# Deformable 3x3 convolution: offsets in 27 products over four strips, four sampling banks, bias in constant rows

## What is computed

```python
x = x + _L0_conv_ref(_gn(x), Wa, ba, Wb, bb, Wg, bg, Wo, bo)
x = x + _L1_conv_ref(_gn(x), w_off, b_off, w_def)
# _L1_conv_ref(x, w_off, b_off, w_def), K = 3, so 9 taps and 18 offsets:
x = jax.nn.relu(x)
offset = conv3x3(x, w_off) + b_off[None, :, None, None]
py = base_y + off[:, :, 0]          # off = offset as (B, 9, 2, H, W)
px = base_x + off[:, :, 1]
samp = _bilinear_gather(x, py, px)  # every tap of every pixel at its own place
out = einsum('bckhw,ock->bohw', samp, w_def)
```

## Time and profile before

| | before |
|---|---|
| median of 3 runs | 1659.01 us (1657.56 to 1660.0) |
| profiled execution, its own time | 1660.34 us |
| its span | 1658.2 us |
| PE busy | 1566.1 us (94%) |
| DVE, ACT, POOL busy | 1183.6, 1033.9, 919.9 us |
| mean granted clock of PE, share of full | 0.982 |

### The profile page before, as it was taken

How to read it: one execution, slowest core, us unless ns; L and a number is a source line. 1 busy time by engine, 2 the same in 40 slices (tenths; PEclk the granted TensorE clock), 3 DMA queues, 4 the chain that set the end, 5 groups by cost and what they waited for, 6 DMA issues and landing times.

```text
span 1658.2 us, 27065 instructions
## 1 busy us (share of the span) xinstructions
PE 1566.1 (94%) x8915; PEld 987.9 (60%) x8916; DVE 1183.6 (71%) x2218; ACT 1033.9 (62%) x1820; POOL 919.9 (55%) x555
## 2 busy tenths in 40 slices
PE   5999999948999999999999999999999999999998
PEld 3778787714555555555555555555555555555554
DVE  5888888745667777776777767777766777767764
ACT  2555555535666666666666666666666666666663
POOL 3555555616555555555555555555555555555561
PEclk9999999958999999999999999999999999999999
DMA  5333333245766666666666666666666666665550
GB/s 145 99 117 117 117 114 114 76 149 167 213 186 180 177 177 177 176 180 179 180 180 183 184 177 176 193 177 184 183 186 180 178 184 182 181 181 171 166 153 26
DMA packets 190601, 268.03 MB, mean 162 GB/s; under 512 B 19710, under 2 KB 128279, under 8 KB 190487
## 3 DMA queue, kind: packets, MB, share of 16 engines
q1 hardware_dynamic: 190486, 266.60, 55.0%
HBM read 188.33 MB, written 78.18 MB: 161 GB/s over the span
## 4 chain that ended last, share of the span: by engine, by line
PE 72%; issue 11%; POOL 6%; DVE 4%; SPq 3%; ACT 3%; DMA 1%; POOLq 0%; DVEq 0%; ACTq 0%
PE bank L827 29%; PE pair L796 22%; PE pair L873 9%; POOL samples_hi L1567 4%; PE pair L845 4%; PE bank L845 3%; DVE samples_lo L1359 2%; ACT samples_hi L1048 2%; PE pair L809 2%; PE pair L811 2%; POOL rstd L1542 1%; POOL samples_lo L1554 1%; SPq L490 0%; POOL weights L1619 0%; PE bank L704 0%
## 5 line engine op out<-in xcount | busy, mean ns | idle before, releaser
L1619 POOL TENSOR_TENSOR weights<-hy_all,hx_all 112x768 f32<-112x768 f32 x384 | 736.8, 1955 | 550.2 <-PE bank L827 507.0
L1359 DVE SCALAR_TENSOR_TENSOR samples_lo<-bank,samples_hi 128x288 f16<-128x288 f32 (+1 forms) x1024 | 450.7, 463 | 287.0 <-ACT samples_hi L1048 281.4
L827 PE MATMUL bank<-weights,zT 112*128 112x288 f32 (+1 forms) x2176 | 616.8, 408 | 24.2 <-DVE samples_lo L1359 24.0
L1048 ACT ACTIVATE samples_hi<-bank 128x288 f16<-128x288 f32 (+1 forms) x1024 | 413.6, 418 | 360.7 <-PE bank L827 330.3
L827 PEld LDWEIGHTS bank<-weights,zT 112*128 112x128 f32 x2176 | 374.5, 190 | 186.7 <-DVE samples_lo L1359 74.0
L796 PE MATMUL pair<-samples_hi,w_hi 128*128 128x512 f16 x576 | 218.8, 380 | 1.3 <-DVE samples_lo L1359 1.3
L796 PE MATMUL pair<-samples_lo,w_hi 128*128 128x512 f16 x576 | 217.5, 378 | 0.0
L796 PE MATMUL pair<-samples_hi,w_lo 128*128 128x512 f16 x576 | 217.4, 377 | 0.0
L1554 POOL TENSOR_TENSOR samples_lo<-samples_hi,samples_lo 128x512 f16<-128x512 f32 x64 | 74.2, 1159 | 130.1 <-ACT samples_lo L959 130.0
L950 ACT ACTIVATE samples_hi<-pair,nbias,rstd 128x512 f32<-128x512 f32 x64 | 49.8, 777 | 154.7 <-PE pair L695 97.5
L1336 DVE TENSOR_TENSOR offs_lo<-offs,offs_hi 114x512 f16<-114x512 f32 x64 | 135.3, 2113 | 2.2
(11 more groups left out here) (139 smaller groups left out, 1962.4 us busy)
## 6 DMA issues: line engine op xcount, KB each, us to landing
hy_all<-hat_y SPq DMA_DIRECT2D x384, 192.0 KB
hx_all<-hat_x SPq DMA_DIRECT2D x384, 192.0 KB
hat_y<-hats SPq DMA_DIRECT2D x256, 126.0 KB
raw<-x_pad SPq DMA_DIRECT2D x68, 272.0 KB, 4.4
x_pad<-hy_all SPq DMA_DIRECT2D x64, 272.0 KB, 3.3
weights<-in_x SPq DMA_DIRECT2D x64, 256.0 KB, 3.0
out<-y SPq DMA_DIRECT2D x32, 512.0 KB, 3.6
hat_x<-hats SPq DMA_DIRECT2D x128, 72.0 KB
```

The lines of the kernel that those rows point to most:

```text
L827: mm = nc.tensor.matmul(sampled_step(n, p)[:, :, c0 - first:c1 - first], zT[0:WPIX, u * WINDOWS + w, :], weights[0:WPIX, u, :, c0:c1], sta ...
L1048: nc.scalar.activation(samples_hi[:, u, :, c0:c1], sampled_step(n, p), ACT.Copy).then_inc(samples_ready, 1)
L1359: nc.vector.scalar_tensor_tensor(out=samples_lo[:, u, :, c0:c1], in0=sampled_step(n, p), scalar=1.0, in1=samples_hi[:, u, :, c0:c1], op0=A ...
L1619: nc.gpsimd.tensor_tensor(to, hy_all[0:WPIX, i * TROWS:(i + 1) * TROWS, :], hx_all[0:WPIX, i * TROWS:(i + 1) * TROWS, :], ALU.mult).then_i ...
```

## The change

1. The offset convolution takes 27 products of 32 stationary columns in place of 9 of 64 and 9 of 32. They go round the four 32-column strips of the array, three rounds of nine taps (z_hi by the high weights, z_hi by the low, z_lo by the high). The wait for z_lo now stands ahead of the first product. The products read the patch with columns outside and 8 rows inside (runs of 8 float16); before, it was read half by half, in runs of 4.
2. offs_hi and offs_lo therefore hold the pixels in the order column, row. The order by halves, which the rest wants, is made in locate, whose four products now read them in runs of 4 where they read 512 in a row before.
3. ACT writes offs_hi straight from PSUM with the scale and no bias; DVE makes offs_lo from PSUM in one instruction. offs4 and the semaphore off_evicted go.
4. The offsets' bias moves into three more constant rows of select (rows 119 to 121), the three float16 parts of the bias. POOL makes them in groups 0 to 4 of the first layer from b_off, which SP loads; SP places them at group 7. Three more rows of ones are loaded.
5. Sampling goes round banks 4 to 7, and a step waits for the samples_lo of four steps before. The turned windows have bank 3 alone, so each group of T waits for the copy of the group just before.

```diff
-        offs4 = sb("offs4", [P, BW])
-        B_OFF, B_CONV, B_ZT, B_S = 0, 2, (3, 4), (5, 6, 7)
+        B_OFF, B_CONV, B_ZT, B_S = 0, 2, 3, (4, 5, 6, 7)
...
+            for i in range(BIAS_PARTS):
+                sp.dma_start(ramps[BIAS_AT + i:BIAS_AT + i + 1, :],
+                             coords_d[0:1]).then_inc(in_select, 16)
...
+            sp.wait_ge(bias_set, 1)
+            sp.dma_start(bias_row[:, P + RAW_AT:P + CONST_AT],
+                         b_off.rearrange("(p a) -> p a", p=1)).then_inc(in_bias, 16)
...
+                by_half = "p (w h r) -> p h w r"
                 for axis in range(2):
-                    nc.tensor.matmul(pairs[0][:, axis, :], select[:, axis, :],
-                                     offs_hi[:], start=True, stop=False)
-                    mm = nc.tensor.matmul(pairs[0][:, axis, :], select[0:CONST_AT, axis, :],
-                                          offs_lo[0:CONST_AT, :], start=False, stop=True)
+                    to = pairs[0][:, axis, :].rearrange("p (h w r) -> p h w r", h=2, r=HR)
+                    nc.tensor.matmul(to, select[:, axis, :],
+                                     offs_hi[:].rearrange(by_half, h=2, r=HR),
+                                     start=True, stop=False)
+                    mm = nc.tensor.matmul(to, select[0:CONST_AT, axis, :],
+                                          offs_lo[0:CONST_AT, :].rearrange(by_half, h=2, r=HR),
+                                          start=False, stop=True)
...
-                wait(pe, lows_ready, STEPS * n + p - 2)
+                wait(pe, lows_ready, STEPS * n + p + 1 - len(B_S))
...
-                products = [(z_hi, k, 2 * 32, k % 2 * 64) for k in range(TAPS)]
-                products += [(z_lo, k, 32, (64, 0, 96, 32)[k % 4]) for k in range(TAPS)]
-                for i, (pixels, k, width, at) in enumerate(products):
-                    if i == TAPS:
-                        pe.wait_ge(z_lo_ready, n + 1)
+                q = 4
+                pe.wait_ge(z_lo_ready, n + 1)
+                for i in range(3 * TAPS):
+                    k, at = i % TAPS, i % q * 32
+                    pixels, w = ((z_hi, woff_hi), (z_hi, woff_lo), (z_lo, woff_hi))[i // TAPS]
                     ky, kx = k // 3, k % 3
                     mm = nc.tensor.matmul(
-                        bank[B_OFF][at:at + width, :].rearrange("p (h w r) -> p h w r", h=2, r=HR),
-                        woff[:, k, 0:width],
-                        pixels[:, kx:kx + UW, ky:ky + BR].rearrange("p w (h r) -> p h w r", h=2),
-                        start=(i < 2), stop=(i + 4 >= len(products)), tile_position=(0, at))
+                        bank[B_OFF][at:at + 32, :].rearrange("p (w r) -> p w r", r=BR),
+                        w[:, k, :], pixels[:, kx:kx + UW, ky:ky + BR],
+                        start=(i < q), stop=(i + q >= 3 * TAPS), tile_position=(0, at))
...
-                nc.scalar.activation(offs4[0:CONST_AT, :], bank[B_OFF][0:CONST_AT, :], ACT.Identity,
-                                     bias=bias_off[0:CONST_AT, :],
-                                     scale=unscale[0:CONST_AT, OFF:OFF + 1]
-                                     ).then_inc(off_evicted, 1)
+                nc.scalar.activation(
+                    offs_hi[0:CONST_AT, :],
+                    bank[B_OFF][0:CONST_AT, :], ACT.Copy,
+                    scale=unscale[0:CONST_AT, OFF:OFF + 1]).then_inc(off_high, 1)
...
-                nc.vector.tensor_copy(offs_hi[0:CONST_AT, :], offs4[0:CONST_AT, :]
-                                      ).then_inc(off_high, 1)
-                dve.wait_ge(off_high, n + 1)
-                nc.vector.tensor_tensor(offs_lo[0:CONST_AT, :], offs4[0:CONST_AT, :],
-                                        offs_hi[0:CONST_AT, :], ALU.subtract).then_inc(off_split, 1)
+                nc.vector.scalar_tensor_tensor(
+                    out=offs_lo[0:CONST_AT, :],
+                    in0=bank[B_OFF][0:CONST_AT, :],
+                    scalar=unscale[0:CONST_AT, OFF:OFF + 1],
+                    in1=offs_hi[0:CONST_AT, :],
+                    op0=ALU.mult, op1=ALU.subtract).then_inc(off_split, 1)
...
+                    pool.wait_ge(in_bias, 16)
...
+                if isinstance(g, int) and g < 5:
+                    split_bias(g)
```

More of the change, by code:

```diff
@@ L61 @@
 CONST_AT = RAW_AT + NOFF
-SUM_ROWS = CONST_AT + 2 + RAMPS
+BIAS_AT = CONST_AT + 2 + RAMPS
+BIAS_PARTS = 3
+SUM_ROWS = BIAS_AT + BIAS_PARTS
 TROWS = 3
@@ L67 @@
 IN_OFF = 16 * 3
-IN_SELECT, SELECT_STEPS = 16 * 29, 8
+IN_SELECT, SELECT_STEPS = 16 * (29 + BIAS_PARTS), 8
+BIAS_STEPS = 8
 BAND_STEPS, ROW_STEPS = 12, 2 + 4 * TAPS
@@ L236, in preact_conv_kernel @@
         y = sb("y", [P, 2, BR * WW])
+        bias_row, bias_rest = (y[0:1, 0, i * 2 * P:(i + 1) * 2 * P] for i in range(2))
+        bias_parts = (y[0:1, 1, :].bitcast(F16)[:, 0:BIAS_PARTS * 2 * P]
+                      .rearrange("p (i c) -> p i c", i=BIAS_PARTS))
         far_band = sb("far_band", [BANDS, 1])
@@ L262, in preact_conv_kernel @@
         in_select = sem("in_select")
+        in_bias = sem("in_bias")
+        bias_set = sem("bias_set")
+        bias_placed = sem("bias_placed")
         select_set = sem("select_set")
@@ L406, in sampled_step @@
             first, end = step_columns(p)
-            return (bank[B_S[(STEPS * n + p) % 3]][:, 0:2 * TAPS * (end - first)]
+            return (bank[B_S[(STEPS * n + p) % len(B_S)]][:, 0:2 * TAPS * (end - first)]
                     .rearrange("p (k c) -> p k c", k=2 * TAPS))
@@ L490, in load_ramp @@
                     sp.dma_start(
-                        ramps[row:row + 1, :].rearrange("p (h w r) -> p h w r", h=2, r=HR)
+                        ramps[row:row + 1, :].rearrange("p (w h r) -> p h w r", h=2, r=HR)
                         [:, h, columns],
@@ L544, in group @@
                                  ).then_inc(in_select, 16)
+                if isinstance(g, int) and g == 7:
+                    sp.wait_ge(bias_set, BIAS_STEPS)
+                    for i in range(BIAS_PARTS):
+                        sp.dma_start(select[BIAS_AT + i:BIAS_AT + i + 1],
+                                     bias_parts[:, i].rearrange("p (a c) -> p a c", a=2)
+                                     ).then_inc(bias_placed, 16)
                 if not isinstance(g, int) or g + XR < GROUPS:
@@ L837, in turn_windows @@
                     wait(pe, zT_a, zT_copied(n, 0)[0] - 1)
-                elif g == 1:
-                    wait(pe, zT_v, zT_copied(n, 1)[1] - 1)
-                else:
-                    a, v = zT_copied(n, g - 2)
-                    pe.wait_ge(*((zT_a, a) if g % 2 == 0 else (zT_v, v)))
+                else:
+                    a, v = zT_copied(n, g - 1)
+                    pe.wait_ge(*((zT_a, a) if g % 2 == 1 else (zT_v, v)))
                 ws = range(4 * g, min(4 * g + 4, WINDOWS))
@@ L845, in turn_windows @@
                     mm = nc.tensor.transpose(
-                        bank[B_ZT[g % 2]][0:WPIX, (w % 4) * P:(w % 4 + 1) * P],
+                        bank[B_ZT][0:WPIX, (w % 4) * P:(w % 4 + 1) * P],
                         z[:, u, w].rearrange("p r c -> p (r c)"),
@@ L1030, in evict_offsets @@
                 act.wait_ge(off_done, n + 1)
-                wait(act, off_split, n)
-                nc.scalar.activation(offs4[0:CONST_AT, :], bank[B_OFF][0:CONST_AT, :], ACT.Identity,
-                                     bias=bias_off[0:CONST_AT, :],
-                                     scale=unscale[0:CONST_AT, OFF:OFF + 1]
-                                     ).then_inc(off_evicted, 1)
+                wait(act, located, n)
+                nc.scalar.activation(
+                    offs_hi[0:CONST_AT, :],
+                    bank[B_OFF][0:CONST_AT, :], ACT.Copy,
+                    scale=unscale[0:CONST_AT, OFF:OFF + 1]).then_inc(off_high, 1)
             def distances(n, u, _):
@@ L1058, in copy_windows @@
                 nc.scalar.copy(zT[0:WPIX, at:at + c, :].rearrange("p w c -> p (w c)"),
-                               bank[B_ZT[0]][0:WPIX, 0:c * P]).then_inc(zT_a, 1)
+                               bank[B_ZT][0:WPIX, 0:c * P]).then_inc(zT_a, 1)
             act.wait_ge(select_set, SELECT_STEPS)
@@ L1379, in copy_windows @@
                 nc.vector.tensor_copy(zT[0:WPIX, at:at + c, :].rearrange("p w c -> p (w c)"),
-                                      bank[B_ZT[1]][0:WPIX, 0:c * P]).then_inc(zT_v, 1)
+                                      bank[B_ZT][0:WPIX, 0:c * P]).then_inc(zT_v, 1)
             def add_x1(n, u, k):
@@ L1557, in _, with split_bias @@
             low_x(0)
+            def split_bias(step):
+                if step == 0:
+                    pool.wait_ge(in_bias, 16)
+                    of = bias_row[:, P + RAW_AT:P + CONST_AT]
+                    nc.gpsimd.tensor_copy(
+                        bias_row[:, 0:Y_ROWS].rearrange("p (g o k) -> p g o k", g=TROWS, k=TROWS),
```

(13 more changed lines are left out.)

7 lines of the change are left out of this document (4 added, 3 removed).

## The result

The changed kernel takes 1632.24 us (median of 4 runs, 1631.51 to 1636.86) beside 1658.28 for the kernel before (1656.14 to 1660.0): ratio 0.9849, 95% interval 0.9827 to 0.9872. It is 1.5% faster, clear of the spread of the runs, as forecast (1635.0, 1616 to 1655). The profiled execution took 1631.68 us with a span of 1629.9 us, against a span of 1658.2 before: 28.3 us less.

What follows compares the result with a forecast made beforehand. PE, in order, was taken to bound the kernel (72% of the chain). Usual bands -35.8, slow ones +9.2, last three -1.7, fill +1.2, start +3: -24.1 from 1660.34, less 1.3 for the median: 1635 us, range 1616 to 1655.

Steps and rivals of the forecast that it cites:

- Rival A: The main forecast: -0.73 us in a usual band, +0.92 in a slow one, 1635 us in all; chance 0.42.
- C: Runs of 8 cost half the surplus (waves of 0.25 us) and locate pays: -0.49 a band, 1649 us; chance 0.16.
- D: Waves of 0.216 us and locate free: -1.00 a usual band, +0.65 a slow one, 1619 us; chance 0.12.
- Parts 1 and 2: Four banks take off 0.56 us at s2, but O then waits for z_lo: only 0.12 a band is left.
- Part 3: O's 27 products make seven waves of 0.216 us: 1.61 against 2.49, -0.88 a band; -0.40 at the other end.
- Hidden where a run streams in 3.3 ns: In O, reading costs 2.2 ns a run, hidden at 3.3 ns streaming, so runs of 8 give waves of 0.216 us.
- Part 4: Locate's four products, now reading runs of 4, take 0.285 us each instead of 0.215: +0.27 a band.
- Part 5: DVE's offs_lo falls from 2.18 us to some 0.7, but PE does not wait for it: zero.
- The sum of a band: Banks and wait -0.12, O -0.88, locate +0.27: -0.73 us a band.
- Part 6: Ten bands whose patch wraps, with z_lo behind POOL's third piece, get 0.92 us longer including locate; nothing for the clock.
- Rival E: z_lo loses the race with POOL's third piece in every band: all 59 pay +0.92, 1716 us; chance 0.09.
- Part 7: Outside the repeated bands: last three bands -1.7 us, fill +1.2, start of the first layer +3 for late loads and bias.

Runs made afterwards that it cites:

- at 32 bytes: Changed kernel with O reading runs of 4 float16 again, plus rows of z_hi and z_lo 32 bytes apart instead of 20: 1665.8 us, ratio 1.0047.
- the old split: Changed kernel with the offsets split as before (ACT writes f32 to SBUF, DVE copies the high part and subtracts): 1635.38 us, ratio 0.9865.

## Why the prediction was right

The forecast of -24.1 against -28.3 by the spans, point by point in the order of its parts. Rival A is what happened in its order of events. Of its two prices, a wave came out between A's and C's, and locate almost free, as in D.

**Parts 1 and 2, banks and wait.** Right: the stall at s2 went, and 0.12 of 0.56 was to be left. 0.04 was: from the first product of s15 to O it is 911.72 - 906.21 = 5.51 instead of 5.55 (923.69 - 918.14). The mis-sized term is the hand-over: 0.06 was taken from s2, and it is 892.59 - 892.44 = 0.15 here. With three banks and the rest of the change a band takes 0.03 more, which is the fourth bank's worth within this change. That four banks alone bring 34 us on the kernel before (1660.97 - 1626.7) shows what the wait at the head of O took.

**Part 3, O.** 2.49 to 1.78 where 1.61 was said: -0.71, not -0.88. The direction and its reason hold, since in runs of 4 O would be 2.09, the figure that the prediction gave for waves at 0.285. The step that was off is 0.216 for a wave in runs of 8. In the records of single products the first starts at 892.587 and the seventh wave at 893.990, so a wave took 1.403 / 6 = 0.234, and the way out 0.38 and not 0.31. "Hidden where a run streams in 3.3 ns" is the sentence that fails: runs of 8 at 2.4 GHz are hidden for two rows of the kernel (0.38) and not for the middle one (0.43).

**Part 4, locate.** +0.27 was expected, +0.04 came (0.229 a product for 0.218). The step "in runs of 4 each takes 0.285 by the same reading" fails: the price is not one of the run. Locate's runs of 4 all start at byte 0 or 8 of their 16, and so do those of the first row at 32 bytes, which were cheap too (405 ns); those of O at 20 bytes start at other places as well and pay. The Trainium skill (SBUF — State Buffer, Door 1: The DMA port swizzle) says that reads keep their rate while two hits fall in a 16-byte line. Locate, four hits in each line, agrees within 0.01 us a product; rival D had this half right. The products of O in runs of 4 don't agree: at 20 bytes those of the first row never hit a line only once and yet last 447 ns (the first three of a band) instead of 380, and at 32 bytes those of the last row neither, and last 511.

**Part 5, the parts from PSUM.** Right: zero in the bands, with four banks. With three it may not be, as the next part shows.

**The sum of a band.** 0.04 + 0.71 - 0.04 = 0.71 of the measured 0.76. The other 0.05 was not foreseen: one product of sampling shortly ahead of locate, where DVE ran its 2.9 us of split offsets, took 0.29 us to the next on average over 58 bands, and takes 0.24 now. Four banks alone take this away, and so do three banks with the short split. That fits a sampling step that waited for a bank because DVE was late with a low part, but no run shows that wait by itself. Parts 3 and 4 were mis-sized by 0.17 and 0.23 in opposite directions. That -0.73 came within 0.03 of -0.76 is partly luck.

**Part 6, the slow bands.** Right in number and size: ten, 20.88 against 19.93, +0.95 for +0.92. The reason held too when it was tested: with POOL's third piece behind z_lo 1.51 of the 1.74 us of surplus went (20.88 to 19.37, beside 19.14). The Trainium skill (SBUF — State Buffer, Who interferes with whom) says that a DVE instruction with two SBUF inputs and a GpSimd one that reads SBUF lock each other out; the trace agrees, 0.85 alone and 2.36 behind POOL. Rival E (z_lo loses in all bands) didn't come: z_lo starts at 891.60 and wins in 49. "I put nothing on the clock" was off once or twice. After the two slow bands at 717.00 and 737.88 the granted clock was 0.76 and 0.82 in the windows shown above, and the next period was 20.72, 1.6 us over the usual. The O of band 63 shows it as well (2.36 long, at a granted clock of 0.73 from 1553 to 1557 us). Behind the other eight idle stretches of 2 us the bands keep their 19.14 and 20.88. In the traces of the four experiments that keep such stretches, ten each, a drop to a granted clock of 0.50 follows one of them three times with runs of 4, three times with runs of 4 at 32 bytes, once with the old split and never with three banks: nine in fifty. In the runs without them the clock stays full in the bands.

**Part 7, once.** +3 for the start of the first layer was too much. POOL did wait for the bias, and PE for POOL, as said:

```profile
31.68 0.41 SPq L537 DMA_DIRECT2D y<-in_b_off  x1
...
35.09 1.71 SPq L466 DMA_DIRECT2D weights<-in_x  x2
...
33.07 0.28 POOL L1588 COPY y<-y 1x126 f32<-1x126 f32 x1 [7.62 <-DMA y<-in_b_off]
...
35.17 0.61 PE L756 MATMUL pair<-samples_lo,abg_space 128*128 128x512 f16 x1 [5.64 <-POOL samples_lo L1578]
```

But the x loads left at 35.09, not later than the 35.48 of the earlier trace rows: the issues ahead of them ran shorter. The three constant rows (0.83) and the ramps (7.55) together take what the ramps alone took before (8.44), and the select rows behind them take 5.95 instead of 6.71, which covers the bias. The idle 6.57 us ahead of 41.76 had room for the groups that came late. In band 0 the products that read z_lo started at 347.71; all of O starts at 348.70 now, 0.99 later. The fill, +1.2, gave back 2.06 by band 5 instead. By band 5 the prediction's terms make +3 + 1.2 - 0.73 = +3.5 and the measured is -1.1. That is 4.5 too much, and it is the distance between -24.1 and -28.3 but for 0.3 at the end, where O of band 63 lost to the clock. Why the fill gave back 2 us was not tested, but for the f16 parts: with the old split it loses them again (3.3 at band 5). The clock bears on it too. From 396 to 403 us, ahead of O of band 4, the kernel before and the changed one show:

```profile
396.00:403.00 7.00, 5.50 (x13) 3.90 (x14) 4.67 (x9) 3.04 (x6) 1.52 (x2) 0.52 0.64 150
396.00:403.00 7.00, 5.41 (x27) 3.42 (x26) 4.84 (x9) 4.50 (x10) 1.85 (x2) 1.00 0.56 130
```

The kernel before ran there at half the clock, and so did the old split for half as long; the changed kernel ran at the full one. The prediction priced no clock in the fill. Whether the clock fell there because of the changed order or by chance is not shown, so part of these 4.5 us may be chance.

**The conclusion that the prediction left unsaid.** Its own terms showed a wait moved ahead of 18 products that do not need it, for up to 0.46 us in 49 bands and 2 us in ten. Undoing that alone was worth 41 us, more than the change itself.

## What to carry to other kernels

When several loads of work are merged into one loop, put each wait ahead of the first instruction that reads what it waits for, not ahead of the loop: here that one line was worth 41 us, and the whole change 26. Where a short instruction and a long one of another engine race for a port with 0.1 us between them, order them by a wait, on the side that nobody waits for. Test the parts of a change alone: the four banks, applied alone to the kernel before, beat the whole change.
